# A four-phase transformer block on one core: four row buffers in the expert phases, a moved row step in the mixing phase, a reordered attention batch, and ring slots loaded by one transfer each

## The reference

```python
x = x + attention(layernorm(x))      # elu(x@qk_w + b) + 1, rope, 8 heads of linear attention, plus a 3-tap convolution
x = x + experts(layernorm(x))
x = x + mix(layernorm(x))            # RWKV: k, v, r products, a recurrence over the tokens, w_output; then relu(.)^2 channel mixing
x = x + experts(layernorm(x))        # the same weights once more

def experts(x):                      # 4096 tokens, 8 experts, top 2
    scores = softmax(x @ gate_w.T)
    # each token's two best experts e: out += score_e * (silu(x @ w1[e]) * (x @ w3[e])) @ w2[e]
```

## Time and profile before

| | us |
|---|---|
| median of 3 runs | 1770.49 |
| profiled execution, its own time | 1768.61 |
| its span, first to last instruction | 1766.8 |
| busy: PE / PEld / DVE / POOL / ACT | 1411.7 / 1187.6 / 1016.4 / 785.0 / 615.4 |
| mean granted TensorE clock | 0.873 of full speed |
| DMA | 157.63 MB, mean 89 GB/s |

### The profile page before, as it was taken

One profiled execution on the slowest core, in us unless ns is written; L12 is line 12 of the kernel. 1 busy time (PEld: TensorE's weight loads), 2 busy tenths in 40 slices (PEclk: granted clock), 3 DMA queues, 4 the chain that ended last, 5 costly groups with the idle time before them and its releaser, 6 DMA issues. The chain is left out here.

```text
span 1766.8 us, 28651 instructions
## 1 busy us (share of the span) xinstructions
PE 1411.7 (80%) x7528; PEld 1187.6 (67%) x7529; DVE 1016.4 (58%) x2226; ACT 615.4 (35%) x1400; POOL 785.0 (44%) x608
## 2 busy tenths in 40 slices
PE   5999974899999994378495867748774799999997
PEld 5888874688888884155364554536564578888886
DVE  5756656344444442798866868595634444444443
ACT  3555643222323332342424324233432223233332
POOL 4555633344545553443533436162323245445553
PEclk9888885899999997689697888878886799999999
DMA  6646462755543334200000000000000854643332
GB/s 203 219 157 213 156 239 100 235 122 120 137 109 56 55 54 111 85 1 12 13 12 12 12 12 12 24 0 25 13 25 24 303 146 101 153 92 54 54 54 42
DMA packets 100857, 157.63 MB, mean 89 GB/s; under 512 B 10256, under 2 KB 60688, under 8 KB 100816
## 3 DMA queue, kind: packets, MB, share of 16 engines
q1 hardware_dynamic: 73120, 118.67, 19.7%
q0 software_dynamic: 27264, 37.82, 13.0%
q10 hardware_dynamic: 432, 0.66, 0.2%
HBM read 95.89 MB, written 61.21 MB: 89 GB/s over the span
## 5 line engine op out<-in xcount | busy, mean ns | idle before, releaser
L1756 PE MATMUL bank<-b_fv,b_hT 128*128 128x256 f32 x512 | 123.6, 403 | 88.5 <-ACT b_hT L1374 88.5
L924 POOL DMA_INDIRECT x_rows<-first_y,first_add_token x71 | 112.6, 1586 | 167.5 <-DMA x_rows<-first_y,first_add_token 67.3
L924 POOL DMA_INDIRECT out_x<-second_y,second_add_token x71 | 112.5, 1585 | 166.9 <-DMA out_x<-second_y,second_add_token 59.5
L1756 PEld LDWEIGHTS bank<-b_fv,b_hT 128*128 128x128 f32 x512 | 103.7, 204 | 107.1 <-ACT b_hT L1374 91.6
L1075 DVE TENSOR_TENSOR second_hT_lo<-bank,second_hT_hi 128x512 fp32r<-128x512 f32 x71 | 49.1, 692 | 166.5 <-ACT second_hT_hi L958 157.3
L1075 DVE TENSOR_TENSOR first_hT_lo<-bank,first_hT_hi 128x512 fp32r<-128x512 f32 x71 | 49.1, 692 | 162.1 <-ACT first_hT_hi L958 152.9
L153 PE MATMUL bank<-second_ring,second_xT_hi 128*128 x284 | 120.0, 423 | 2.2 <-DVE second_xT_lo L1063 2.2
L153 PE MATMUL bank<-first_ring,first_xT_hi 128*128 x284 | 119.7, 422 | 2.2 <-DVE first_xT_lo L1063 2.2
L155 PE MATMUL bank<-second_ring,second_xT_lo 128*128 x284 | 113.1, 398 | 0.0
L154 PE MATMUL bank<-first_ring,first_xT_hi 128*128 x284 | 112.9, 397 | 0.0
L155 PE MATMUL bank<-first_ring,first_xT_lo 128*128 x284 | 112.8, 397 | 0.0
(11 more groups left out here) (354 smaller groups left out, 4193.1 us busy)
## 6 DMA issues: line engine op xcount, KB each, us to landing
first_ring<-split_weights SPq DMA_DIRECT2D x96, 256.0 KB
second_ring<-split_weights SPq DMA_DIRECT2D x96, 256.0 KB
a_wraw<-in_L_ffn_w SPq DMA_DIRECT2D x24, 512.0 KB, 4.4
split_weights<-a_whi SPq DMA_DIRECT2D x24, 512.0 KB, 2.7
split_weights<-a_wlo SPq DMA_DIRECT2D x24, 512.0 KB, 3.8
normed_rows<-xg SPq DMA_DIRECT2D x16, 528.0 KB, 3.0
x_rows<-x SPq DMA_DIRECT2D x8, 512.0 KB, 5.0
x<-x_rows SPq DMA_DIRECT2D x8, 512.0 KB, 9.3
```

Of the source, the lines that this page charges most:

```text
L924: nc.gpsimd.indirect_dma_start(x_dram[:], bass.IndirectOffsetOnAxis(ap=add_token[par][:], axis=0), y[par][:], None, compute_op=ALU.add).th ...
L1756: last = nc.tensor.matmul(out[:, j * C:(j + 1) * C], src(i, j), w[:, i, :], start=(i == 0), stop=(i == chunks - 1))
```

## The change

Four groups of edits.

- Attention. The weight pieces have three buffers instead of two; all three loads stand at the top of SP's batch, and the third piece's high part (ACT) and low part (DVE) move to before the evacuation of the next batch's transposes. The statistics and the square root of `x` are made two batches ahead, in the middle of the batch, and ACT's normalise of the next batch opens its batch. PE runs the gate transposes after tap 0 of tile 2, the gate products after taps 1 and 2 of it, and puts tap 0 of tile 3 behind the gate products and tap 1 behind the `kz` products. The batch loop's last three bodies are written out.
- Experts, rows. `xs`, `y` and the token columns have four buffers instead of two (the `y` buffers lie in tables no longer needed). Three gathers are issued at the start, gather(i+3) in step i; an evacuation of y waits for the add four blocks before. The loop is unrolled by four.
- Experts, ring. A slot is loaded by one transfer of 3 MB; only slot 0 is loaded at the start, slots 1 to 3 once block 1 is transposed.
- Mix. `row_finish(b)` moves from behind m = 6 to the end of ACT's batch.

```diff
 def over_batches(engine, body):
 
     body(0, 0)
-    with engine.Fori(1, B - 2, 2) as b:
+    with engine.Fori(1, B - 4, 2) as b:
         body(b, 1)
         body(b + 1, 0)
+    body(B - 3, 1)
+    body(B - 2, 0)
     body(B - 1, 1)
...
@@ phase_attention: buffers, SP
-        wraw = [sb(f"a_wraw{i}", [P, PIECE]) for i in range(2)]
...
+        wraw = [sb(f"a_wraw{i}", [P, PIECE]) for i in range(3)]
+        whi = [sb(f"a_whi{i}", [P, PIECE], F32R) for i in range(3)]
+        wlo = [sb(f"a_wlo{i}", [P, PIECE], F32R) for i in range(3)]
...
             def period(b, par):
-                load_piece(b, par, 0)
-                load_piece(b, par, 1)
+                for n in range(3):
+                    load_piece(b, n)
                 if not is_first(b):
                     store_x(b - 1)
-                store_piece(b, par, 0)
-                load_piece(b, par, 2)
-                store_piece(b, par, 1)
+                store_piece(b, 0)
+                store_piece(b, 1)
+                store_piece(b, 2)
                 if not is_first(b):
                     store_rows(b - 1)
-                store_piece(b, par, 2)
...
@@ phase_attention: ACT period
+                if not is_last(b):
+                    act.wait_ge(rstd_ready, b + 2)
+                    wait_count(act, kv_done, b)
+                    normalise(xn[1 - par], mv, shift, b + 1, xn_ready)
                 wait_count(act, q_ready, b)
                 for n, m in enumerate(ORDER):
...
                 if not is_first(b):
                     route_before(b)
-                if not is_last(b):
-                    act.wait_ge(rstd_ready, b + 2)
-                    normalise(xn[1 - par], mv, shift, b + 1, xn_ready)
-                high_part(b, par, 0)
+                high_part(b, 0)
...
                 if not is_first(b):
                     row_exp(b)
+                high_part(b, 2)
                 if not is_last(b):
                     evacuate_next(round_next(b), 1 - par)
                 if not is_first(b):
                     row_finish(b)
-                high_part(b, par, 2)
...
@@ phase_attention: POOL (rstd of x(b+2) behind add_bias(b+1)) and DVE
             def period(b, par):
                 own.round(b + 1)
-                if not is_last(b):
-                    wait_apart(pool, var_ready, b + 2, passed["pool"])
-                    rstd(mv, shift, rstd_ready)
...
+                if has_second(b):
+                    wait_apart(pool, var_ready, b + 3, passed["pool"])
+                    rstd(mv, shift, rstd_ready)
...
-                if not is_last(b):
-                    statistics(bn, mv, b + 1, var_ready)
...
-                weight_low(b, par, 0)
+                weight_low(b, 0)
+                if has_second(b):
+                    dve.wait_ge(x_in, 16)
+                    wait_apart(dve, xn_ready, b + 2, passed["dve"])
+                    statistics(bn, mv, b + 2, var_ready)
...
                 own.link(nc.vector.reciprocal(zr[:], zr[:]))
+                weight_low(b, 2)
                 if not is_last(b):
                     low_part(b + 1, 1 - par)
...
-                weight_low(b, par, 2)
...
@@ phase_attention: PE
                 convolution(par, 0)
                 convolution(par, 1)
-                convolution(par, 2)
+                convolution(par, 2, (0,))
                 if not is_first(b):
                     gate_transposes(b)
-                convolution(par, 3, (0, 1))
+                convolution(par, 2, (1, 2))
                 if not is_first(b):
                     gate_products(b)
+                convolution(par, 3, (0,))
...
                 last.then_inc(z_done, 1)
+                convolution(par, 3, (1,))
                 pe.wait_ge(t_emptied, round_k(b) + 1)
...
@@ over_blocks, phase_experts
-    assert NBLK % 2 == 1
-    for i in range(3):
-        body(i, i % 2)
-    with engine.Fori(3, NBLK - 3, 2) as i:
-        body(i, 1)
-        body(i + 1, 0)
-    for i in range(NBLK - 2, NBLK):
-        body(i, i % 2)
+    assert NBLK % 4 == 3
+    for i in range(7):
+        body(i, i % 4)
+    with engine.Fori(7, NBLK - 7, 4) as i:
+        for n in range(4):
+            body(i + n, (3 + n) % 4)
+    for i in range(NBLK - 4, NBLK):
+        body(i, i % 4)
...
-        xs = [sb(f"xs{i}", [P, RW]) for i in range(2)]
+        xs = [sb(f"xs{i}", [P, RW]) for i in range(NX)]
...
-        y = [sb(f"y{i}", [P, C]) for i in range(2)]
...
+        homes = [chosen[:].rearrange("p k e t -> p (k e t)")] + [t[:].rearrange("p k j b -> p (k j b)") for t in block_hot]
+        y = [t[:, 0:C] for t in homes]
+        gather_token = [sb(f"gather_token{i}", [P, 1], U32) for i in range(NX)]
+        add_token = [sb(f"add_token{i}", [P, 1], U32) for i in range(NX)]
@@ SP
-                for piece in range(6):
-                    for half in range(2):
-                        part = slice(half * PIECE // 2, (half + 1) * PIECE // 2)
-                        sp.dma_start(ring[:, n % NS, piece, part].bitcast(F32),
-                                     split[:, piece, part].bitcast(F32)).then_inc(slot_in[n % NS], 16)
+                sp.dma_start(ring[:, n % NS, :, :].bitcast(F32), split.bitcast(F32)).then_inc(slot_in[n % NS], 16)
...
             load(0)
-            load(1)
             announce(0)
-            announce(1)
             sp.wait_ge(xt_done, 2)
-            for n in range(2, NS):
+            for n in range(1, NS):
                 load(n)
-            for n in range(2, NS):
+            for n in range(1, NS):
                 announce(n)
@@ POOL
-                if isinstance(i, int) and i < 2:
+                if isinstance(i, int) and i < NX:
                     pool.wait_ge(token_ready, i + 1)
                 else:
-                    pool.wait_ge(row_used, i - 1)
+                    pool.wait_ge(row_used, i - NX + 1)
...
-            gather(0, 0)
-            gather(1, 1)
+            for i in range(NX - 1):
+                gather(i, i)
             pool.wait_ge(x_stored, 16 * B)
...
-                if not (isinstance(i, int) and i >= NBLK - 2):
-                    gather(i + 2, par)
+                if not (isinstance(i, int) and i > NBLK - NX):
+                    gather(i + NX - 1, (q + NX - 1) % NX)
                 if not is_first(i):
-                    add(i - 1, 1 - par)
+                    add(i - 1, (q - 1) % NX)
@@ ACT
-                if not (isinstance(i, int) and i < 2):
-                    act.wait_ge(added, 16 * (i - 1))
+                if not (isinstance(i, int) and i < NX):
+                    act.wait_ge(added, 16 * (i - NX + 1))
...
@@ phase_mix: ACT
                     if not static(b, 0) and m == 2:
                         row_exp(b)
-                    if not static(b, 0) and m == 6:
-                        row_finish(b)
...
                 if has_next(b, 2):
                     evacuate_xn(b + 2)
+                if not static(b, 0):
+                    row_finish(b)
```

More of the change, by code:

```diff
@@ L309, in phase_attention, with has_second @@
                                                                   sem("a_total_ready"), sem("a_row_ready"))
-        wraw_in = [sem(f"a_wraw_in{i}") for i in range(2)]
+        wraw_in = [sem(f"a_wraw_in{i}") for i in range(3)]
         whi_ready, wlo_ready = sem("a_whi_ready"), sem("a_wlo_ready")
-        w_stored = [sem(f"a_w_stored{i}") for i in range(2)]
+        w_stored = [sem(f"a_w_stored{i}") for i in range(3)]
         block = ctx.enter_context(nc.Block())
+        def has_second(b):
+            return not (isinstance(b, int) and b + 2 >= B)
         def round_gate(b):
@@ L382, in _ @@
             store_rows(B - 1)
-            sp.wait_ge(w_stored[0], 32 * (3 * B // 2))
-            sp.wait_ge(w_stored[1], 32 * (3 * B // 2))
+            for n in range(3):
+                sp.wait_ge(w_stored[n], 32 * B)
         @block.scalar
@@ L501, in _ @@
             add_bias(0)
+            pool.wait_ge(var_ready, 2)
+            rstd(mv, shift, rstd_ready)
             own.pad()
@@ L598, in period @@
                 own.round(b + 1)
-                if isinstance(b, int) and b == 1 or not isinstance(b, int):
-                    dve.wait_ge(x_in, 16)
-                if not is_last(b):
-                    statistics(bn, mv, b + 1, var_ready)
                 if not is_first(b):
@@ L833, in phase_experts @@
         w_ready, w_given, row_used = sem("w_ready"), sem("w_given"), sem("row_used")
-        loaded = [sem(f"loaded{i}") for i in range(2)]
+        loaded = [sem(f"loaded{i}") for i in range(NX)]
         added = sem("added")
@@ L975, in _, with step @@
             give_weights(0)
-            def step(i, par):
+            def step(i, q):
+                par = q % 2
                 if not (isinstance(i, int) and i < 2):
-                    evacuate_y(i - 2, par)
+                    evacuate_y(i - 2, (q - 2) % NX)
                 act.wait_ge(a_done, i + 1)
@@ L1040, in _ @@
```

(5 more changed lines are left out.)

87 lines of the change are left out of this document (39 added, 48 removed).

## The result

| | before | after |
|---|---|---|
| median, us | 1769.93 (4 runs, 1768.41 to 1777.91) | 1688.01 (4 runs, 1684.91 to 1690.2) |
| ratio | | 0.953 (0.950 to 0.9555) |
| profiled execution: its own time, span | 1768.6, 1766.8 | 1690.2, 1688.4 |

What follows compares the result with a forecast made beforehand. Expert loops are near PE's pace, the mix is held by a circle of waits, attention by PE's clock. 1768.6 - 63.7 (mix) - 0 - 12 (attention) - 6 (experts) = 1686.9; median 1.9 above: 1689 us, range 1650 to 1736.

Steps and rivals of the forecast that it cites:

- Mix: Mix: moving ACT's row step to its batch's end removes the stall before hT 7; -63.7 us.
- the lower bound's mechanism: Mix: PE idles for gT instead and its clock falls there, losing 2 us a batch again; gain only 52 us.
- Attention waits: Attention: third weight buffer, earlier statistics and moved normalise hide beside PE; by waits the change is 0.
- the 1.27 us wait keeps its cover of 12 matmuls: Attention: PE's 1.27 us wait for the evacuated gate rows still has 12 matmuls covering it, so it stays.
- Clock: Attention: convolution products around key transposes to kv products lift PE's granted clock; -12 us, between 0 and -29.
- the bound of -29: Attention: PE's clock never falls over key transposes to kv products, saving 4.2 us in each of seven batches.
- Experts, the rows: Expert loops: four row buffers give gathers and adds more slack; with the ring, -3 us a phase, -6 in all.
- The lower bound: Expert phase: adds still lose 3.5 us each to loads, so it ends at 676, 10 us better than 686.2.
- PE then need not wait for either: Expert loops: with four row buffers PE waits neither for gathers nor for y's adds; no separate size.
- Experts, the ring: Expert loops: one transfer a slot still takes 12 us; the earlier start gives 1.8 us a phase.
- The term without a row: Expert loops: what an add loses to a load, some 3.5 us before, with no profile row for the changed ring.
- the first rival: Expert loops: whole-slot loads block small transfers, adds lose 6 to 10 us; experts +16 to +64, total 1711 to 1759; 24%.

Runs made afterwards that it cites:

- a_mixback: The changed kernel with ACT's row step (`row_finish`) back behind hT 6 in the mix; 1747.4 us.
- a_convback: The changed kernel with attention's convolution products in the order of before, weight buffers and ACT's order as changed; 1708.2 us.
- b_conv: The kernel before with only the order of attention's convolution products changed as in the change; 1773.1 us (ratio 0.999).
- b_rows4: The kernel before with only the four row buffers, each ring slot still loaded by twelve transfers; 1759.7 us (ratio 0.992).
- The run of one part undone: The changed kernel with each ring slot loaded by twelve transfers of 2 KB rows again, load order and four row buffers kept; 1665.6 us.
- c_paced: The changed kernel with twelve transfers a slot, slot 1 loaded behind the first transposes, slots from 2 on loaded piece by piece; 1646.6 us.

## Why the prediction was right or wrong

**Mix, right.** -63.4 against -63.7, and a_mixback gives it to the row step alone. That the two agree so closely is in part luck, since within it two errors cancel. Five cycles gained 10.3 to 11.2 us (53.1 in all against 57.2): the full ones stopped at 68.1 to 68.2 us instead of the 67.20 us of batch 0. And the end behind the last gT gained 9.4 where 5.6 + 0.9 stood. PE's idle before gT was forecast as the lower bound's mechanism. It came, and at a lower clock (539 ns for one product with `w_output`, 427 before), but cost less than the 2 us a batch allowed for it.

**Attention waits, wrong.** The step of the prediction that failed: "the 1.27 us wait keeps its cover of 12 matmuls". The cover was not what ended it. PE's gate transposes and ACT before, batch 1, and ACT after:

```profile
56.28 1.09 PE L672 MATMUL bank<-ident,xg 128*128 128x128 f32 x8
...
54.06 2.08 ACT L427 ACTIVATE xg<-x,a_shift,a_mv 128x256 f32 x4 [2.91 <-POOL a_shift L490]
56.05 2.07 ACT L427 ACTIVATE a_xn<-x,a_shift,a_mv 128x256 f32 x4
58.02 1.04 ACT L423 ACTIVATE a_whi<-a_wraw 128x1024 fp32r<-128x1024 f32 x1
58.97 1.05 ACT L403 ACTIVATE a_xgT<-bank 128x512 f32<-128x512 f32 x2
```

```profile
63.41 2.08 ACT L427 ACTIVATE xg<-x,a_shift,a_mv 128x256 f32 x4 [1.74 <-POOL a_shift L491]
65.39 1.04 ACT L423 ACTIVATE a_whi<-a_wraw 128x1024 fp32r<-128x1024 f32 x1
66.74 1.08 ACT L404 ACTIVATE a_xgT<-bank 128x512 f32<-128x512 f32 x2 [0.31 <-PE bank L676]
```

The 2.07 us normalise of the next batch stood between the rows and their evacuation; before, PE's transposes ended at 57.37, and the evacuation began at 58.97 without idle, so ACT was late, not PE's transposes. The normalise was moved away, and I priced that as hidden. The 1.3 us went in the six batches that had them (1 to 6; batch 7 had no such wait before), and they are gone in a_convback too, where the order of the products is the old one. The normalise was not moved alone in any run. The forecast of 0 by waits is off by little all the same: of the some 8 us of idle that the other edits took in a_convback, only 2.5 remain as a gain in the change, where PE waits 5.7 us for the keys in batch 0.

**Clock, mis-sized.** -12 was taken, with "The idle and the gate products still adjoin". They did not, as just shown. The measured term is PE's busy time, -25.7 us, more than twice the -12. The runs together, by the first table product: the other edits alone 7 to 13 us (a_convback), both 28 to 38, while the order alone gave nothing to the kernel's time (b_conv). The order pays only with the other edits, which took away the waits ahead of the gate products and left the one for `xg` at 0.3 us or less a batch. Had the wait been read right, the same argument would have led near the bound of -29.

**Experts, the rows: right.** Four buffers alone gave 13 us (b_rows4). The lower bound had rows and the earlier start together at 10 us a phase with an unchanged loss of an add, 1.8 of it the start, so some 16 us for the rows. But "PE then need not wait for either" went too far: b_rows4 still has 7.7 us of waits for gathers behind the first block of the first phase, 13.2 before.

**Experts, the ring: wrong.** The term without a row was taken at the price of the twelve transfers, 3.5 us an add; it is 5.6 to 7.6 for a single load and 9.4 for the three in a row. So -6 was forecast for rows and ring together, and tables and steps measured +11.8. That is the first rival's mechanism, at a total a little below its foot of +16: the adds of a phase spread over 369.4 and 370.2 us, at the 370 above which the prediction called itself wrong (passed by 0.2 us in the second phase). The run of one part undone prices it at 22 us. The Trainium skill (DMA: Bandwidth & Descriptors, "Queues, rings and completion order") has an engine turn between queues only at packet boundaries; that an add loses more as rows grow from 2 to 8 to 24 KB fits it, but no run shows what such a packet is here, and the loss is far from proportional to the row. The Trainium skill (the same page, "Rules for kernel authors") wants small transfers made one large one: here a load by itself became 1.3 us shorter (10.8 against 12.1), and the kernel lost 22 us to the small transfers beside it.

The total was right by luck: attention gave 16 us more than forecast and the experts took 18 more, and the two errors cancel.

## What to carry to other kernels

A bulk load with deadlines far away should be slow: split, and issued piece by piece, it let a latency-bound chain of small transfers run at its own pace (-19 us), where one large transfer cost 22. When a wait is taken out of a circle of waits, look at once for the gaps of the next engine: two moved steps on DVE gave 22 us more. And the instruction that ends a wait must be followed one further back: the 1.3 us came from what stood ahead of it on its own engine.

## What the runs showed of the hardware

- A granted clock of 0.50 and 1.00 (1.2 and 2.4 GHz) over the same products depends on what stands ahead of them. With gate products, key transposes and kz products in one row and only 0.29 to 0.38 us of idle among them it fell (a_convback); with six full products behind the gate products it stayed up in batches 1 to 7 (after); with the same six, but 1.4 to 1.9 us of idle ahead of the gate transposes and 0.5 to 1.3 us ahead of the gate products, it fell in batches 1 to 6, once so early that all gate products ran slow (3.58 us instead of 1.85 in b_conv).
- An accumulating indirect DMA of 128 rows of 1 KB, 3.8 us alone, makes the next start 3 us late behind a 3 MB load in rows of 2 KB, 5 in rows of 8 KB, 7 in rows of 24 KB, and at most 1.3 in the first phase of c_paced, where only 256 KB of a load are under way.
